# TensorE's order in the first layer of a four-layer graph network: count steps between halves of the turns and look-ups, target sums last

## The reference, cut to what matters

```
r1 = r[a[:, 0]] * e                                  # a = (src, dst) of each edge, e its features
r2 = r[a[:, 1]] * e
out = segment_sum(r1, a[:, 1]) + segment_sum(r2, a[:, 0])
x = layernorm(x + out)
```

## Time and profile before

| | us |
|---|---|
| median of 3 runs (2379.21 to 2386.02) | 2382.91 |
| the profiled execution, its time | 2381.67 |
| the profiled execution, its span | 2379.6 |
| loop turns 1 to 10 of the first layer, with count steps | about 222 to 1130 in the span |

### The profile page before, as it was taken

The page is one execution under the profiler, slowest core; times in us unless marked ns, Lnnn a source line. Parts: engine busy times, 40 slices in busy tenths (PEclk is TensorE's granted clock), DMA queues, the critical chain, the costliest instruction groups (busy, mean ns, idle before and its releaser), DMA issues.

```text
span 2379.6 us, 41543 instructions
## 1 busy us (share of the span) xinstructions
PE 1549.5 (65%) x7809; PEld 1069.1 (45%) x7813; DVE 1394.0 (59%) x4832; ACT 714.3 (30%) x1272; POOL 1342.8 (56%) x1329
## 2 busy tenths in 40 slices
PE   3135777766776777776888544665556653796994
PEld 3034444444443444443777523554445553453552
DVE  8636766766766766777677755545555455425224
ACT  0001555554554555555000012222122221231230
POOL 0067777777777777777777437777777771000000
PEclk9978666666666666665899765656556566898997
DMA  1333444444444444444898422222222222232320
GB/s 44 70 91 93 128 122 121 125 117 117 126 125 117 129 124 116 127 131 128 220 250 230 130 53 54 53 53 52 52 52 54 51 51 106 97 148 94 145 97 27
DMA packets 332397, 251.06 MB, mean 106 GB/s; under 512 B 105217, under 2 KB 306541, under 8 KB 328619
## 3 DMA queue, kind: packets, MB, share of 16 engines
q1 hardware_dynamic: 224523, 118.11, 17.9%
q0 software_dynamic: 42240, 86.08, 13.5%
q10 hardware_dynamic: 65440, 45.04, 6.0%
HBM read 172.45 MB, written 78.22 MB: 105 GB/s over the span
## 4 chain that ended last, share of the span: by engine, by line
PE 36%; POOL 20%; issue 14%; DVE 10%; ACT 4%; DMA 3%; ACTq 2%; DVEq 2%; SPq 1%; POOLq 0%
POOL shared L822 18%; PE PS L999 11%; PE PS L899 8%; PE PS L872 6%; PE PS L884 4%; ACT PS L1158 3%; PE PS L863 2%; DMA shared<-record 2%; POOL G L810 2%; DVE shared L1621 2%; DVE shared L1560 2%; ACT shared L1164 1%; ACTq L1171 1%; DVE X L1681 1%; SPq L684 1%
## 5 line engine op out<-in xcount | busy, mean ns | idle before, releaser
L796 POOL DMA_INDIRECT record<-shared,IX x440 | 457.9, 1041 | 185.0 <-issue 161.5
L822 POOL DMA_INDIRECT shared<-table,src_of x440 | 439.6, 999 | 188.1 <-issue 133.8
L899 PE MATMUL PS<-shared 128*128 128x400 bf16 x816 | 298.9, 463 | 181.9 <-ACT PS L1158 154.7
L782 POOL DMA_INDIRECT G<-in_x_dram,MET x264 | 269.3, 1020 | 200.3 <-DMA MET<-meta_d 120.1
L1158 ACT ACTIVATE PS<-PS,kept 128x400 f32<-128x400 f32 x407 | 231.0, 568 | 221.9 <-PE PS L899 207.6
L1164 ACT ACTIVATE shared<-PS 128x400 uint16<-128x400 f32 x408 | 205.5, 504 | 125.8 <-issue 124.5
L1621 DVE TENSOR_SCALAR shared<-iota_h,shared 128x400 bf16<-128x400 f16 x816 | 238.2, 333 | 0.0
L1079 PE MATMUL PS<-shared,G 128*128 128x128 f32 x880 | 213.3, 389 | 18.2 <-issue 6.9
L872 PE MATMUL PS<-X,OHT 128*128 x880 | 207.0, 410 | 4.4 <-issue 2.6
L872 PEld LDWEIGHTS PS<-X,OHT 128*128 128x128 f32 x880 | 180.8, 306 | 64.3 <-issue 64.3
L899 PEld LDWEIGHTS PS<-shared 128*128 128x128 bf16 x816 | 64.0, 108 | 317.4 <-issue 200.7
(11 more groups left out here) (326 smaller groups left out, 2343.0 us busy)
## 6 DMA issues: line engine op xcount, KB each, us to landing
nearby<-shared ACTq DMA_DIRECT2D x408, 100.0 KB
shared<-in_edge_attr_dram SPq DMA_DIRECT2D x616, 64.0 KB
shared<-nearby SPq DMA_DIRECT2D x28, 1400.0 KB, 8.6
shared<-record SPq DMA_DIRECT2D x110, 258.0 KB, 3.4
MET<-meta_d SPq DMA_DIRECT2D x440, 2.0 KB
record<-shared,IX POOLq DMA_INDIRECT x440
shared<-table,src_of POOLq DMA_INDIRECT x440
G<-in_x_dram,MET POOLq DMA_INDIRECT x264
```

What stands on the lines that cost most here:

```text
L782: pool.indirect_dma_start(G[:, d, j, 0:D], None, x[:, :], row_index(MET[:, q, j, SRC - D:SRC - D + 1].bitcast(U32))).then_inc(a.gather[d], 16)
L796: pool.indirect_dma_start(record2[:, :], row_index(IX[:, q, j:j + 1]), M[:, g, j, :], None, bounds_check=SLOTS - 1, oob_is_err=False).then ...
L822: pool.indirect_dma_start(G2[:, half, GROUP * q + j, :], None, table1[:, :], row_index(src_of[:, GROUP * n + j:GROUP * n + j + 1])).then_i ...
L899: t = pe.matmul(PS[:, bank_, 0:HI], LOW[:, g, h, :], VIN[:, g, h, :], start=False, stop=h == 1, skip_group_check=True)
```

## The change

```diff
-                for j in range(GROUP):
+                for j in range(GROUP // 2):
+                    pe.transpose(PS[:, g, j * P:(j + 1) * P], OH[:, q % DEEP, j, :], ident[:, :])
+
+            def turn_a_rest(i, q):
+                g = q % SIDES
+                for j in range(GROUP // 2, GROUP):
                     t = pe.transpose(PS[:, g, j * P:(j + 1) * P], OH[:, q % DEEP, j, :], ident[:, :])
                 t.then_inc(a.turned, 1)
 
+            look_regs = []
+
             def look_up(i, q):
                 g, n = q % SIDES, group(i, q)
-                regs = columns(PE, columns_of[0], n)
+                look_regs[:] = columns(PE, columns_of[0], n)
                 pe.wait_ge(a.onehot_t, n + 1)
                 freed(pe, s_m2, i, q, SIDES)
-                for j in range(GROUP):
+                for j in range(GROUP // 2):
+                    pe.matmul(PS[:, 2 + g, j * P:(j + 1) * P], OHT[:, g, j * P:(j + 1) * P],
+                              X[:, bass.ds(look_regs[j], D)], start=True, stop=True)
+
+            def look_up_rest(i, q):
+                g = q % SIDES
+                for j in range(GROUP // 2, GROUP):
                     t = pe.matmul(PS[:, 2 + g, j * P:(j + 1) * P], OHT[:, g, j * P:(j + 1) * P],
-                                  X[:, bass.ds(regs[j], D)], start=True, stop=True)
+                                  X[:, bass.ds(look_regs[j], D)], start=True, stop=True)
                 t.then_inc(a.looked, 1)
...
-            pipeline(pe, (turn_a, 2), (step_pe(0), 0), (look_up, 1), (step_pe(1), 0), (sum_a, 0), (step_pe(2), 0), (step_pe(3), 0),
+            pipeline(pe, (turn_a, 2), (step_pe(0), 0), (turn_a_rest, 2), (step_pe(1), 0), (look_up, 1), (step_pe(2), 0),
+                     (look_up_rest, 1), (step_pe(3), 0), (sum_a, 0),
                      (prepare_pe, 0))
```

## The result

The changed kernel takes 2494.02 us (median of 4 runs, 2488.55 to 2503.66) against 2381.06 us for the kernel before (4 runs beside it, 2368.6 to 2386.02): ratio 1.0484, 95% interval 1.0448 to 1.0519. It is slower by 113 us; the forecast's sum was +111 (118 - 7).

The account below looks back on a forecast made before the run. No engine is full; a chain running from engine to engine sets the pace. 2381.67 + 118 (groups' new waits, less clock give-back) - 7 (loop-turn starts) = 2493, 2494 with the median; range 2437 to 2542.

Parts of the forecast that it names:

- The sum: Whole kernel: 2381.67 + 118 for the groups - 7 for loop-turn starts = 2493, with 1.2 to the median 2494.
- Wait A: TensorE before step 3: DVE builds its operands behind source messages that await the look-up's second half; about 1.6 us a group.
- Wait B: TensorE before step 1: ACT's copy, ahead of that step's seed, waits for the late turned matrices; 1.36 us idle.
- The two cycles: One group at TensorE's lower clock: F (with target sums) 11.0 us against 9.88, L (without) 9.65 against 7.3.
- 0.42 given back: TensorE at the higher clock 20 to 25% of the time: a quarter of 160 to 170 us returned, 42 in all.
- The clock: TensorE's granted clock: waits cut its work into pieces, so the mean stays low, 0.58 to 0.62 in 100 us windows.
- Where a loop turn begins: ACT's standstill before the copy is partly hidden behind its wait for the turns: 0.7 us in 10 turns, -7 us.
- The signs named ahead: Profile after: L1635 waits 100 us and more, none before target sums, ACT's copy waiting for turns, ACT x88 to x90.
- R1: Rival, chance 0.05: TensorE's clock stays up at 1.00 between short waits; 2365 to 2385 us.
- R2: Rival, chance 0.03: step 3's operands are mostly ready on DVE, so no wait there; faster, 2330 to 2365 us.
- R3: Rival, chance 0.04: DVE late in F groups, one-hots and step 2's build behind the addition to `acc`; +30 more, 2525 to 2555.

Follow-up runs that it names:

- the one order that was tested: Kernel before with DVE's target rows ahead of the source messages: 2341.00 us; with a fifth gather added in each F group: 2412.98 us.

## Why the prediction was right, point by point

**The sum.** Forecast 2494, measured 2494.02. The mechanism was right in the main, but this agreement is luck: the terms were off in ways that cancelled. Over the profile the groups were to cost 118 us, the starts of loop turns -7 and the rest nothing, 111 in all. By the mean cycles the groups cost 93 (59 F and 39 L cycles), the starts of loop turns +12, and 9 lie before the first and behind the last of these cycles, 114 in all. The median of the kernel before also came out 2 us lower than the one that the sum started from.

**Wait A** was right in cause, place and size: a wait of about 1.6 us was forecast once a group, and 1.58 to 1.89 stood before all 99 steps 3. Its removal gave 131 us against the 128 that the same cycle gave, with a part in it that belongs to the clock.

**Wait B** is there with about its size (1.38 to 1.50 against 1.36), but the step "*New wait B* ... now `turned` comes only after step 0 and two more turns" named the wrong cause. Whole turns changed 4 us. In L groups it is ACT's own list between step 3 and step 1, which the cycle had as coming at the same time ("ACT is free ... too"). In two thirds of the F groups it is DVE, whose build of step 1 stands behind the addition to `acc`; I had priced that at 5.4 against 5.7 after step 3 and dismissed it ("DVE isn't the limit in this"). A difference of 0.3 us was no ground for that: taking away the two together is worth 100 us, clock included, and neither alone over 38.

**The two cycles.** The F group above, mostly at the lower clock, takes 10.71 (11.0 forecast) and the L group 9.38 (9.65). On the mean, each with 0.42 given back, I had +0.7 for F (1.1 - 0.42) and +1.9 for L (2.35 - 0.42); the trace has +0.39 and +1.80. L groups do lose most; the F group was forecast too long.

**The clock** behaved about as argued: 0.60 to 0.64 in windows of 100 us from 300 to 1100, against 0.58 to 0.62 forecast, and 0.64 in the earlier trace rows. It neither stayed up nor paid for the longer groups. The Trainium skill's page "TensorE: Matmul & The Clock Gate" (section "Part 1: The HAM clock gate") says that the throttled clock is the default and that activity releases it. Read as a promise that a TensorE with only short waits keeps its clock up, it would have given no loss. The trace is against that reading: in the L group above no wait is longer than 1.59 us, and the granted clock is 0.50 from its start to its end.

**Where a loop turn begins** I forecast -0.7 us and the trace has a cost instead: those cycles, F cycles too, grew by 1.70 us where the others grew by 0.39, about 1.3 x 9 = 12 us. ACT's stop isn't hidden behind the wait for the turns. TensorE's timeline of the changed kernel shows two waits in a row there, first 2.99 us for ACT, then 0.99 for DVE, which stood still as well:

```profile
529.67 0.83 PE L912 MATMUL PS<-shared 128*128 128x400 bf16 x2 [2.99 <-ACT PS L1172]
...
532.72 0.85 PE L912 MATMUL PS<-shared 128*128 128x400 bf16 x2 [0.99 <-DVE shared L1635]
```

**The signs named ahead** were seen: waits on line 1635 (188.2 us from 300 to 1100, over the 100 named, since step 1's are among them), none before the sums to speak of, ACT's copy behind TensorE's turns (71.1 us), ACT x87 to x90 in 100 us.

**The rivals.** R1 fell with the clock. R2 fell with wait A, which is in every group. R3, DVE late behind the addition, came true in part: the addition does delay DVE's builds. But what it holds is step 1, which R3 didn't name, and step 2 by only 0.18 us in the row at 543.28; and this hold takes the place of ACT's and doesn't come on top.

## What to carry to other kernels

When work is moved into another engine's gaps, what decides is what stands ahead of the answer on the neighbours' in-order lists: which of their stages each moved piece releases, and which it then waits for. Here one exchange on DVE's list turned a loss of 113 us into a gain of 18, and with a second on ACT's list into 35.
When a step has two requirements that come within some tenths of a microsecond of each other, both must be priced and removed together: 38 and 14 us alone were 100 together.
If several different orders stop at the same time, look for the engine with the steady list; here POOL's indirect transfers, at some 1.33 us each, are the floor of the one order that was tested, at 2341 us.

## What the runs showed of the hardware that was not expected

Where a loop turn begins, ACT and DVE each stand still for about three microseconds without anything that the profile shows them to wait for, in both kernels (before, ACT 3.22 to 3.49 and DVE 2.44 to 3.08 us in eight loop turns). In the changed kernel, ACT's copy and DVE's one-hots at that place:

```profile
528.47 0.60 ACT L1162 ACTIVATE OHT<-PS 128x512 f32<-128x512 f32 x1 [3.29 <-issue]
...
530.98 0.88 DVE L1554 TENSOR_SCALAR shared<-iota,DL 128x128 f32<-128x128 f32 x4 [2.88 <-issue]
```

DVE's stop ends 2.5 us after ACT's here, so TensorE waits for one and then for the other (2.99 and 0.99 above). Before, it ended 1.15 to 2.12 us ahead of ACT's, and a loop turn's last cycle was 1.30 us longer than other F cycles, where it is now 2.61. What causes the stops was not tested.
